# Three borders between four programs of a fused decoder: later clearing of semaphores, one meeting of the engines, last stores waited for in the next program

## The chip, the cores and the metric

The kernel runs on one core of a Trainium2 chip. The core has five engines with an instruction stream of their own: PE (matrix products), DVE (vector), ACT (scalar), POOL (GpSimd) and SP, which here only issues DMAs. They agree by semaphores. The metric is the device time of one launch in microseconds (us), median of several runs. Beside it stands one profiled execution, whose span goes from the first to the last instruction on the core.

## The reference

A decoder of two layers on x of 8 x 512 x 256 in float32. Each sublayer is added to its input and normalised:

```python
x = _layernorm(x + _L0_attn_ref(x, ...))    # recurrent mixer with weights mixed by a router
x = _layernorm(x + _L0_xattn_ref(x, ctx_1024, ctx_1024, ...))   # 16 heads, pruned columns
x = _layernorm(x + _L0_ffn_ref(x, ...))     # 8 experts, top 2, capacity 1024
x = _layernorm(x + _L1_attn_ref(x, ...))    # gated linear attention with decay
x = _layernorm(x + _L1_xattn_ref(x, ctx_1024, ctx_1024, mask, ...))
x = _layernorm(x + _L1_ffn_ref(x, ...))     # 8 experts, all computed, weighted by a gate
```

The expert layer writes each token to a slot of a table `buf` of 8 x 1024 rows, runs the experts over the table and gathers two result rows for each token.

## The kernel before

`decoder` runs four programs one after the other: `stage_front` (the mixer of layer 0, and q, k and v of the cross attention), `stage_attend_route` (attention, routing, scatter into `buf`, and a fallback path), `stage_experts` (16 units of 512 table rows) and `stage_tail` (all of layer 1). Tiles and semaphores are named with the prefixes front, xa, ex and ta. Each program is a `Block` with one hand-written instruction stream for each engine. Its streams end in a branch, and the block ends in a **meeting**: every engine drains (waits until its own work is done), reports to POOL, and goes on when POOL releases it. So no engine starts the next program until the last one is there.

A `Room` holds one program's tiles and semaphores. Its `clear` (L30 to L34) is called when the program's context is left, after the block: POOL resets the program's semaphores to zero (L33), and a second meeting of all engines follows (L34). Only then do the streams of the next program start. There are three such borders, and the same two steps once more at the end of the kernel.

SP's stream ends each program with waits on DMAs. What matters here:

- `stage_front`, L226 to L229: the loads `ahead_ld`, the zeroing of `buf` (`zero_st`), the stores of x1 (`x1_st`) and the stores of q, k and v (`qkv_st`). The last q and k parts leave from `w_all`, where the next program keeps the tile `early`; v leaves from `late`.
- `stage_attend_route`, L858 to L862: loads for later (`k_ld`), stores of x2, stores of the fallback rows (`fo_st`, from the tile probs) and POOL's scatters (`sent`).
- `stage_experts`, L1564: the stores of the expert outputs (`st`, 16 units in two buffers) to the table `results`.
- `stage_tail`, L1858: the stores of the output.

The first work behind each border: in the attention program SP loads the second chunk of q and k, L88 (the first lies in `late` already), PE makes scores (L1347), DVE and ACT take maxima and exponentials (L1076, L979), POOL normalises (L909), PE transposes (L1360), and `copy_tile` (L740 on DVE, L742 on ACT) moves the transposed tiles to `early` for the first eight heads. In the expert program PE first makes two weight products (L1689) while SP loads table rows (L1550), x2 and fallback rows of sequence 0 (L1554, L1555). In the tail PE transposes x3 (L2296), SP loads x2 and fallback rows of sequence 1 and the contexts (L1832 to L1838), and POOL gathers the result rows of sequence 1 by eight indirect DMAs (`gather(1)`, L1866).

The order inside each engine's stream is written out by hand; nothing is scheduled.

## Time and profile before

| what | us |
|---|---|
| median of 3 runs | 1961.33 (1960.6 to 1966.12) |
| the profiled execution's own time | 1966.77 |
| its span | 1964.7 |
| PE busy in the span | 1783.4 (91%) |
| DVE busy | 1264.8 (64%) |
| ACT busy | 991.4 (50%) |
| POOL busy | 639.4 (33%) |
| mean granted clock of PE | 0.970 of full |

The profiled execution took 2.1 us more than its span, and 5.4 us more than the median. The borders lie at about 238 to 249, 1011 to 1016 and 1374 to 1380 us. PE is busy nearly all the time between them. Rows that end in a bracket give the idle time before the row and what ended it. A name ending in q (SPq, POOLq) is the sequencer of that engine, where waits, drains and DMA issues are recorded.

### The profile page before, as it was taken

To read this page: it belongs to the slowest core of one execution; us is meant where nothing else is said; L and a number is where in the kernel's file an instruction comes from. 1 tells how busy PE (TensorE), PEld (TensorE's weight loads), DVE (VectorE), ACT (ScalarE), POOL (GpSimd) and SP (SyncE) were. 2 spreads that over 40 slices of the span, in tenths; PEclk is the share of its full clock that TensorE was granted. 3 is DMA by queue.
4 is the path that set the end of the run, shared out by engine and by line. 5 is a ranking of instruction groups with operands and counts; after the bars stand their busy time and mean duration, and the time that the engine had idled before them with its cause. 6 is when DMAs were issued, how large, how long until landed. Compare 5 with 4: busy or idle time off the path is not lost. (4 is left out here: it accounts for less than half of the span.)

```text
span 1964.7 us, 26168 instructions
## 1 busy us (share of the span) xinstructions
PE 1783.4 (91%) x8373; PEld 1058.0 (54%) x8373; DVE 1264.8 (64%) x2933; ACT 991.4 (50%) x2603; POOL 639.4 (33%) x813
## 2 busy tenths in 40 slices
PE   7999868989889898888869999999678999999997
PEld 5556534455445454544445566566455665666553
DVE  2686558888989999898411211221566878786665
ACT  4336689999989898997321111111232333233220
POOL 2000055555667666666310001000541324221100
PEclk9999989999999999999889999999788999999999
DMA  5248821212222222321662334431411111100000
GB/s 215 86 169 277 261 86 44 60 54 70 82 55 83 78 79 66 81 81 65 226 212 82 132 107 139 147 111 54 150 60 59 35 58 49 49 12 17 11 12 21
DMA packets 164071, 183.29 MB, mean 93 GB/s; under 512 B 19652, under 2 KB 143803, under 8 KB 162912
## 3 DMA queue, kind: packets, MB, share of 16 engines
q1 hardware_dynamic: 157792, 165.46, 26.4%
q0 software_dynamic: 6144, 16.18, 2.6%
q8 instruction: 67, 1.10, 0.2%
q14 instruction: 68, 0.56, 0.1%
HBM read 119.01 MB, written 63.18 MB: 93 GB/s over the span
## 5 line engine op out<-in xcount | busy, mean ns | idle before, releaser
L909 POOL TENSOR_SCALAR xa_probs<-xa_probs,xa_small 128x512 f32<-128x512 f32 x512 | 344.8, 690 | 242.0 <-DVE xa_small L1070 241.9
L979 ACT ACTIVATE xa_probs<-xa_ps_s,xa_small 128x512 f32<-128x512 f32 x512 | 360.9, 742 | 40.7 <-DVE xa_small L1076 36.1
L1076 DVE TENSOR_REDUCE xa_small<-xa_ps_s 128x2 f32<-128x1024 f32 x256 | 309.1, 1208 | 41.2 <-PE xa_ps_s L1347 41.2
L1360 PE MATMUL xa_ps_t<-xa_ident,xa_probs 128*128 128x128 f32 x2048 | 308.3, 283 | 17.1 <-DVE early L740 7.1
L1360 PEld LDWEIGHTS xa_ps_t<-xa_ident,xa_probs 128*128 128x128 f32 x2048 | 229.5, 142 | 151.9 <-ACT early L742 44.4
L2442 PE MATMUL ta_ps_e<-late,ta_x5T 128*128 128x512 f32 x512 | 235.8, 594 | 1.4 <-DVE ta_acc L2195 1.4
L1347 PE MATMUL xa_ps_s<-xa_k,xa_q 96*128 96x512 bf16 x496 | 151.4, 387 | 54.0 <-ACT xa_probs L979 52.4
L1610 ACT ACTIVATE ex_hid<-ex_ps_g 128x512 f32<-128x512 f32 x64 | 38.2, 597 | 275.7 <-PE ex_ps_u L1709 272.9
L2195 DVE SCALAR_TENSOR_TENSOR ta_acc<-ta_ps_e,ta_gate,ta_acc 128x256 f32<-128x256 f32 x256 | 123.5, 483 | 67.4 <-PE ta_ps_e L2442 60.8
L1665 DVE TENSOR_TENSOR ex_hid<-ex_hid,ex_ps_u 128x512 f32<-128x512 f32 x64 | 44.0, 687 | 184.5 <-ACT ex_hid L1610 179.0
L2442 PEld LDWEIGHTS ta_ps_e<-late,ta_x5T 128*128 128x128 f32 x512 | 93.9, 189 | 96.8 <-issue 84.0
L742 ACT ACTIVATE early<-xa_ps_t 128x512 f32<-128x512 f32 x216 | 135.4, 652 | 8.1 <-PE xa_ps_t L1360 7.6
L742 ACT ACTIVATE late<-xa_ps_t 128x512 f32<-128x512 f32 x216 | 134.0, 653 | 8.4 <-PE xa_ps_t L1360 8.4
L979 ACT ACTIVATION_READ_ACCUMULATOR xa_probs<-xa_ps_s,xa_small 128x1 f32 x512 | 133.6, 261 | 0.0
L1709 PE MATMUL ex_ps_g<-ex_xsT,early 128*128 128x512 f32 x256 | 121.9, 599 | 2.3 <-ACT ex_xsT L1593 2.3
L1709 PE MATMUL ex_ps_u<-ex_xsT,early 128*128 128x512 f32 x256 | 120.3, 592 | 0.0
L1719 PE MATMUL ex_ps_d<-early,ex_hid 128*128 128x256 f32 x512 | 113.4, 379 | 0.1
L1719 PEld LDWEIGHTS ex_ps_d<-early,ex_hid 128*128 128x128 f32 x512 | 96.0, 190 | 13.3 <-DVE ex_hid L1665 0.5
L1347 PEld LDWEIGHTS xa_ps_s<-xa_k,xa_q 96*128 96x128 bf16 x496 | 33.9, 99 | 125.9 <-ACT xa_probs L979 85.3
L1866 POOL DMA_INDIRECT ta_rows<-scratch_results,route_i x56 | 54.9, 980 | 90.7 <-POOLq L34 74.8
L1674 DVE COPY ex_out<-ex_ps_d 128x1024 f32<-128x1024 f32 x16 | 19.6, 1224 | 98.2 <-PE ex_ps_d L1719 98.2
L1709 PEld LDWEIGHTS ex_ps_u<-ex_xsT,early 128*128 128x128 f32 x256 | 48.8, 191 | 61.6 <-issue 61.6
(371 smaller groups left out, 3047.5 us busy)
## 6 DMA issues: line engine op xcount, KB each, us to landing
scratch_qk_parts<-front_w_all SPq DMA_DIRECT2D x16, 768.0 KB, 5.7
xa_q<-scratch_qk_parts SPq DMA_DIRECT2D x186, 64.0 KB
xa_k<-scratch_qk_parts SPq DMA_DIRECT2D x186, 64.0 KB
scratch_buf<-late SPq DMA_DIRECT2D x8, 1024.0 KB, 5.3
early<-in_L_ffn_Wg SPq DMA_DIRECT2D x16, 512.0 KB
early<-in_L_ffn_Wu SPq DMA_DIRECT2D x16, 512.0 KB
early<-in_L_ffn_Wd SPq DMA_DIRECT2D x16, 512.0 KB
ex_xs<-scratch_buf SPq DMA_DIRECT2D x16, 512.0 KB, 5.3
```

Of the source, the lines that this page charges most:

```text
L742: eng.activation(dst, src, ACT.Copy, accum_out=out).then_inc(copied[t], 1)
L909: ins = pool.tensor_scalar(probs[n % NP][:, t, :], probs[n % NP][:, t, :], rinv[n % 2][:, t:t + 1], 1.0, ALU.mult, ALU.mult)
L979: ins = act.activation(probs[n % NP][:, t, :], ps_s[j][:, t % 2, :], ACT.Exp, bias=nmax[n % 2][:, t:t + 1], accum_out=rsum[n % 2][:, t:t + 1])
L1076: dve.tensor_reduce(nmax[n % 2][:, 2 * j:2 * j + 2], ps_s[j][:, :, :], AX.X, ALU.max, negate=True).then_inc(max_up, 1)
L1347: ins = pe.matmul(ps_s[j][:, t % 2, :], q_[:, n % CH, t * P:(t + 1) * P], keys[:, n % CH, :], start=True, stop=True)
L1360: ins = pe.transpose(ps_t[t % 2][:, i * P:(i + 1) * P], probs[m % NP][:, i, t * P:(t + 1) * P], ident[:, :])
L1665: dve.tensor_tensor(hid[m % 2][:, j, :], hid[m % 2][:, j, :], ps_u[j % 2][:, :], ALU.mult).then_inc(hid_up, 1)
L1709: ins = pe.matmul(ps[:, :], wt[:, h, j * P:(j + 1) * P], xsT[u][:, h, :], start=(h == 0), stop=(h == DH - 1))
L1719: ins = pe.matmul(ps_d[:, t, :], hid[u][:, j, t * P:(t + 1) * P], wd[u][:, j, :], start=(j == 0), stop=(j == FT - 1))
L1866: pool.indirect_dma_start(out=rows[b % 2][:, n, t, :], out_offset=None, in_=a["results"], in_offset=bass.IndirectOffsetOnAxis(ap=route_i[: ...
L2195: dve.scalar_tensor_tensor(acc[c % 2][:, t, :], ps_e[n % 2][:, i, :], gate[c % 2][:, t, e:e + 1], acc[c % 2][:, t, :], ALU.mult, ALU.add). ...
L2442: ins = pe.matmul(ps_e[n % 2][:, :, :].rearrange("p e d -> p (e d)"), x5T[c % 2][:, h, t * P:(t + 1) * P], ew[:, h, e:e + 2, :].rearrange( ...
```

## The change

- `Room` no longer clears on leaving. `clear` only resets the semaphores, with no meeting after it, and is called one program later: POOL clears front's semaphores as its last instruction in the attention program, and the attention program's as its last in the expert program. The tail registers two clears that run when it is left, for its own and for the expert program's semaphores, with no meeting between or behind them.
- SP's last waits on `qkv_st`, `fo_st` and `st` are taken out of the three programs. They stand in the next program ahead of what needs them: `qkv_st` ahead of the first copies to `early` (ACT and DVE, `m == 0`) and ahead of SP's store of `fw`; `fo_st` ahead of SP's load of the fallback rows and ahead of ACT's first Gelu; `result_st` on POOL ahead of `gather(1)`.
- The other waits at the end of the programs stay.

```diff
     def __init__(self, nc, ctx, stage):
         self.nc, self.ctx, self.stage, self.sems = nc, ctx, stage, []
-        ctx.callback(self.clear)
     def clear(self):
         self.nc.clear_and_free_semaphores(self.sems)
-        self.nc.all_engine_barrier()
...
             sp.wait_ge(zero_st, 16 * B)
             for u in range(2):
                 sp.wait_ge(x1_st[u], 16 * B // 2)
-                sp.wait_ge(qkv_st[u], 48 * B // 2)
...
             g, hp = m // HU, m % HU
+            if m == 0:
+                for u in range(2):
+                    eng.wait_ge(k.qkv_st[u], 48 * B // 2)
...
                 if b == 0:
+                    for u in range(2):
+                        sp.wait_ge(k.qkv_st[u], 48 * B // 2)
                     sp.wait_ge(fn_up, 2 * DH)
...
             for u in range(2):
                 sp.wait_ge(x2_st[u], 16 * B // 2)
-                sp.wait_ge(fo_st[u], 16 * B // 2)
                 sp.wait_ge(sent[u], 16 * 2 * T * B // 2)
...
             pool.tensor_copy(k.bvw[:, :, :], col(k.bv[:, :]).to_broadcast([P, DH, P]))
+            k.front.clear()
...
             sp.dma_start(x2[:, :, :], tok(a["x2"][0])).then_inc(x2_ld, 16)
+            for u in range(2):
+                sp.wait_ge(k.fo_st[u], 16 * B // 2)
             sp.dma_start(fb[:, :, :], tok(a["fallback"][0])).then_inc(x2_ld, 16)
...
-            for u in range(2):
-                sp.wait_ge(st[u], 16 * NU // 2)
...
             pool.tensor_tensor(rstd[:, :], ve[:, :], k.mhalf[:, :], ALU.pow).then_inc(m_root, 1)
+            k.attend.clear()
...
                 wait(act, d_up, m - 1)
+                if m == 0:
+                    for u in range(2):
+                        act.wait_ge(k.fo_st[u], 16 * B // 2)
...
         r = Room(nc, ctx, "ta")
+        ctx.callback(k.expert.clear)
+        ctx.callback(r.clear)
...
+            for u in range(2):
+                pool.wait_ge(k.result_st[u], 16 * E)
             gather(1)
```

What stands in a row on the engines. Semaphores of a cleared program are used again, and these lists give a semaphore the name of its first owner: front_x_ld2 and front_x_ld3 are `st` of the expert program, and barrier_..._gather and _release are the two halves of a meeting.

SP at the first border. Before:

```order
L195 DMA scratch_qk_parts<-front_w_all 128x6x512
L198 DMA scratch_v<-late 128x4x256 [waits front_v_up]
L97 UNCONDITIONAL_BRANCH [waits front_qkv_st0,front_x1_st1,front_x1_st0,front_qkv_st1,front_zero_st,front_ahead_ld]
L750 UNCONDITIONAL_BRANCH [waits barrier_Pool_Activation_PE_DVE_SP_release]
L88 DMA xa_q<-scratch_qk_parts 16x4x512 x6
L88 DMA xa_k<-scratch_qk_parts 16x4x512 x6
```

Now:

```order
L195 DMA scratch_qk_parts<-front_w_all 128x6x512
L198 DMA scratch_v<-late 128x4x256 [waits front_v_up]
L95 UNCONDITIONAL_BRANCH [waits front_x1_st0,front_x1_st1,front_zero_st,front_ahead_ld]
L754 UNCONDITIONAL_BRANCH [waits barrier_Pool_Activation_PE_DVE_SP_release]
L86 DMA xa_q<-scratch_qk_parts 16x4x512 x6
L86 DMA xa_k<-scratch_qk_parts 16x4x512 x6
```

The two waits on the q, k and v stores are gone from the branch; no DMA has changed its place.

POOL from the end of the attention program, through the expert program, to the tail's gather (ISA is the clearing of semaphores). Before:

```order
L966 COPY late<-late 128x256
L653 UNCONDITIONAL_BRANCH
L33 ISA [waits barrier_Pool_Activation_PE_DVE_SP_gather]
L1566 UNCONDITIONAL_BRANCH [waits barrier_Pool_Activation_PE_DVE_SP_gather]
...
L1583 TENSOR_TENSOR ex_rstd<-ex_ve,late 128x4 [waits front_inv_up]
L1524 UNCONDITIONAL_BRANCH
L33 ISA [waits barrier_Pool_Activation_PE_DVE_SP_gather]
L1860 UNCONDITIONAL_BRANCH [waits barrier_Pool_Activation_PE_DVE_SP_gather]
L1866 DMA ta_rows<-scratch_results,route_i 128x256 x8
```

Now:

```order
L971 COPY late<-late 128x256
L32 ISA
L652 UNCONDITIONAL_BRANCH
L1574 UNCONDITIONAL_BRANCH [waits barrier_Pool_Activation_PE_DVE_SP_gather]
...
L1591 TENSOR_TENSOR ex_rstd<-ex_ve,late 128x4 [waits front_inv_up]
L32 ISA
L1530 UNCONDITIONAL_BRANCH
L1874 UNCONDITIONAL_BRANCH [waits barrier_Pool_Activation_PE_DVE_SP_gather]
L1880 DMA ta_rows<-scratch_results,route_i 128x256 [waits front_x_ld2,front_x_ld3]
L1880 DMA ta_rows<-scratch_results,route_i 128x256 x7
```

Each clearing has moved from between two meetings to ahead of the only one, and the gather has got the wait on the last result stores.

POOL at the end of the kernel. Before:

```order
L1870 TENSOR_TENSOR ta_rx<-ta_vex,late 128x4 [waits front_k_up]
L1870 TENSOR_TENSOR ta_rg<-ta_veg,late 128x4 [waits ta_g_var] x2
L1750 UNCONDITIONAL_BRANCH
L33 ISA [waits barrier_Pool_Activation_PE_DVE_SP_gather]
```

Now:

```order
L1884 TENSOR_TENSOR ta_rx<-ta_vex,late 128x4 [waits xa_fT_ld1]
L1884 TENSOR_TENSOR ta_rg<-ta_veg,late 128x4 [waits front_x1_st0] x2
L1762 UNCONDITIONAL_BRANCH
L32 ISA [waits barrier_Pool_Activation_PE_DVE_SP_gather]
L32 ISA x2
```

One clearing instruction has become three, since the numbers of the two programs' semaphores no longer lie in one range.

## Rows read from the trace of the kernel before

**Rows 1.** The page, busy time of each engine.

```profile
PE 1783.4 (91%) x8373; PEld 1058.0 (54%) x8373; DVE 1264.8 (64%) x2933; ACT 991.4 (50%) x2603; POOL 639.4 (33%) x813
```

**Rows 2.** Timeline, border 1: start, length, engine, line, what, [idle before it].

```profile
240.33 1.22 DVE L386 TENSOR_TENSOR late<-front_ps_o,late 128x1024 f32<-128x1024 f32 x1
...
241.57 1.11 SPq L198 DMA_DIRECT2D scratch_v<-late  x1
...
249.36 1.87 PE L1347 MATMUL xa_ps_s<-late 96*128 96x512 bf16 x4 [11.56 <-PEq L34]
```

**Rows 3.** Waits of SP's sequencer: us in total, times, longest.

```profile
SPq L229 <- DMA scratch_v<-late: 5.1, 1, 5.1
...
SPq L1564 <- DMA scratch_results<-ex_out: 2.5, 1, 2.5
...
SPq L861 <- DMA scratch_fallback<-xa_probs: 2.4, 1, 2.4
```

**Rows 4.** Source L97, border 1: PE released by the first meeting (ns, start us).

```profile
L97 PEldq EVENT_SEMAPHORE  x1: 51/51/51, 248.4 to 248.4; - x1
```

**Rows 5.** Source L33, all four clearings: ns min/median/max, first and last start us.

```profile
L33 POOLq DRAIN  x4: 113/166/176, 248.4 to 1963.8; - x4
L33 POOLq EVENT_SEMAPHORE_RANGE_CLEAR  x4: 178/407/457, 248.6 to 1964.0; - x4
```

**Rows 6.** Timeline, border 2.

```profile
999.68 12.54 SPq L782 DMA_DIRECT2D scratch_fallback<-xa_probs  x4
...
1016.23 3.75 PE L1689 MATMUL ex_ps_d<-late 128*128 128x256 f32 x8 [5.51 <-PEq L34]
```

**Rows 7.** Source L653, border 2: POOL's drain, PE's release by the first meeting.

```profile
L653 POOLq DRAIN  x1: 6400/6400/6400, 1006.1 to 1006.1; - x1
...
L653 PEldq EVENT_SEMAPHORE  x1: 51/51/51, 1015.2 to 1015.2; - x1
```

**Rows 8.** Timeline, border 3.

```profile
1379.65 1.94 PE L2296 MATMUL ta_ps_w<-late 128*128 128x128 f32 x8 [5.28 <-PEq L34]
1380.34 1.02 POOL L1866 DMA_INDIRECT ta_rows<-scratch_results,route_i  x1 [74.83 <-POOLq L34]
```

**Rows 9.** Source L1524, border 3: PE's release by the first meeting.

```profile
L1524 PEldq EVENT_SEMAPHORE  x1: 51/51/51, 1379.0 to 1379.0; - x1
```

**Rows 10.** Timeline, the tail's first step.

```profile
1390.40 2.35 POOL L1881 TENSOR_TENSOR ta_x3b<-late 128x1024 f32<-128x1024 f32 x1
...
1391.82 1.91 DVE L2075 TENSOR_TENSOR ta_g<-ta_g 128x4 f32<-128x4 f32 x1 [2.72 <-ACT ta_g L1928]
...
1396.64 3.37 DVE L2052 SCALAR_TENSOR_TENSOR ta_z<-ta_rows,route_w,ta_z 128x256 f32<-128x256 f32 x8
```

**Rows 11.** Timeline, the tail's second step.

```profile
1416.47 0.95 POOL L1866 DMA_INDIRECT ta_rows<-scratch_results,route_i  x1 [0.30 <-issue]
...
1419.25 8.93 DVE L2052 SCALAR_TENSOR_TENSOR ta_z<-ta_rows,route_w,ta_z 128x256 f32<-128x256 f32 x8 [7.25 <-DMA ta_rows<-scratch_results,route_i]
...
1428.09 0.15 DVE L2075 TENSOR_TENSOR ta_g<-ta_g 128x4 f32<-128x4 f32 x1
```

**Rows 12.** Windows: length, busy us (instructions) by engine, then PEclk, DMA share, GB/s.

```profile
1020.00:1022.00 2.00, 2.00 (x7) 1.79 (x8) 0.00 (x0) 0.00 (x0) 0.00 (x0) 0.56 1.05 351
1026.00:1028.00 2.00, 0.52 (x5) 0.28 (x3) 0.00 (x0) 2.00 (x10) 0.00 (x0) 1.00 0.00 0
1028.00:1030.00 2.00, 1.20 (x2) 0.71 (x3) 0.00 (x0) 1.94 (x3) 0.00 (x0) 0.64 0.03 8
1441.00:1443.00 2.00, 0.00 (x0) 0.00 (x0) 1.77 (x4) 0.84 (x4) 1.81 (x2) 1.00 0.00 0
```

**Rows 13.** Windows of the attention program's start, same columns.

```profile
261.00:263.00 2.00, 2.00 (x9) 1.47 (x9) 0.82 (x1) 1.38 (x5) 1.29 (x2) 0.50 0.00 0
```

**Rows 14.** Timeline there: first copy to `early`, first scores from the loaded chunk.

```profile
259.75 0.69 DVE L740 TENSOR_SCALAR_CACHE_REDUCE early<-xa_ps_t 128x512 f32<-128x512 f32 x1 [0.36 <-PE xa_ps_t L1360]
...
266.39 0.59 PE L1347 MATMUL xa_ps_s<-xa_k,xa_q 96*128 96x512 bf16 x2 [0.34 <-ACT xa_probs L979]
```

More of the change, by code:

```diff
@@ L88, in load_half, with stage_front @@
         eng.dma_start(dst[g * DK:(g + 1) * DK, :, :], src.rearrange("(h d) s -> d h s", d=DK)).then_inc(done, 16)
-def stage_front(nc, a, late):
+def stage_front(nc, a, late, k):
     KC = P // E
@@ L98, in stage_front @@
         r = Room(nc, ctx, "front")
+        k.front = r
         w_all = r.sb("w_all", [P, B, DH, 3 * D])
@@ L165, in stage_front @@
         ahead_ld = r.sem("ahead_ld")
+        k.qkv_st = qkv_st
         buf = a["buf"].rearrange("(n p r) d -> n p (r d)", p=P, r=2048 // D)
@@ L654, in stage_attend_route @@
         r = Room(nc, ctx, "xa")
+        k.attend = r
         probT = [room[:, :].rearrange("p (j t s) -> p j t s", t=T, s=S) for room in (early, late)]
@@ L721, in stage_attend_route @@
         fo_st = [r.sem(f"fo_st{u}") for u in range(2)]
+        k.fo_st = fo_st
         k_ld, k_pad = r.sem("k_ld"), r.sem("k_pad")
@@ L1525, in stage_experts @@
         r = Room(nc, ctx, "ex")
+        k.expert = r
         xs = [r.sb(f"xs{j}", [P, T, D]) for j in range(3)]
@@ L1539, in stage_experts @@
         st, w_ld = ([r.sem(f"{n}{u}") for u in range(2)] for n in ("st", "w_ld"))
+        k.result_st = st
         t_up, xsT_up, gu_up, gelu_up, hid_up, d_up, out_up = (r.sem(n) for n in
@@ L2534, in decoder @@
         k = Later(nc, ctx, late)
-        stage_front(nc, a, late)
+        stage_front(nc, a, late, k)
         with ExitStack() as inner:
```

## The prediction

> **What bounds the kernel now.** The page comes first: PE is busy for 91% of the span, no other engine for more than 64% [rows 1]. Between the borders some engine is full all the time, so what shortens a border is not filled again from elsewhere, unless a program's first steps absorb it. The timeline then shows three stretches in which PE stands still: 11.56, 5.51 and 5.28 us, 22.4 us together [rows 2, 6, 8]. That is all that a change of the borders can take. Third, SP's waits say what part of each stretch is the landing of the last stores: 5.1, 2.4 and 2.5 us [rows 3]. Last, the first meeting's release and the next program's first instruction give what the clearing and the second meeting cost.
>
> **The second meeting and the clearing.** At border 1 PE is released by the first meeting at 248.4 and starts at 249.36 [rows 4, 2]; at border 2 at 1015.2 and 1016.23 [rows 7, 6]; at border 3 at 1379.0 and 1379.65 [rows 9, 8]. With 0.1 us left for a release and a first instruction, this part gives 0.85, 0.9 and 0.55 us. It goes whole, for nothing runs beside it.
>
> **Border 1, the stores of q, k and v.** SP arrives last: it issues the last store until 241.57 + 1.11 = 242.7 and then waits 5.1 us for landing [rows 2, 3]. The next to arrive is DVE, whose last operation ends at 240.33 + 1.22 = 241.55 [rows 2]. So without the wait SP is still the last, at 242.7, and the whole 5.1 us go. SP's other waits there showed no time. Sum 5.1 + 0.85 = 5.95; with the second landed semaphore's own instruction 6.0.
>
> The wait moves ahead of the first copies to `early`. DVE makes the first at 259.75 [rows 14], 10.4 us after the border; with the border ending at 243.3 that is 253.7, and the stores landed by 242.7 + 5.1 = 247.8. Cover of 5.9 us, so zero wait; ACT's copies stand behind its own waits, and behind them ACT's exponentials of the next head. Two waits each for the three copies on ACT: at most 0.05 us each by the only semaphore row near [rows 4], 0.3 us together; since each is already met, I take 0.1 for all added waits and keep 0.3 as the end.
>
> SP now issues the second q/k chunk (12 loads) at 243.3, behind stores still moving. Before, all DMA was quiet from 261 on [rows 13], at most 11.7 us after the issue, and PE needs the chunk at 266.39, 17.0 us after [rows 14]. If the chunk had to wait for all the rest of the stores (247.8 - 243.3 = 4.5 us), it would be there after 16.2 us: still 0.8 us early. So zero, bounded above by a few tenths to some us if the two streams disturb each other (the rival of the starts).
>
> By the Trainium skill's page "DMA: Bandwidth & Descriptors", section "Queues, rings and completion order", a DMA's completion increment lands only after every earlier write of that DMA engine. This speaks against the change: the chunk cannot be reported before the stores in front of it. That is the 16.2 us just worked out from rows; by the page too the sum stays as it is.
>
> **Border 2, the fallback stores.** Here another engine is close behind. SP issues until 999.68 + 12.54 = 1012.2 [rows 6], and POOL's drain runs from 1006.1 for 6.4 us to 1012.5 [rows 7]. So POOL becomes the last to arrive, and the clearing of front's semaphores now stands in its stream ahead of the meeting: one more drain and a clearing, 0.17 + 0.41 = 0.6 us [rows 5]. POOL is there at 1013.1 instead of SP at about 1014.7: release at about 1013.3 against 1015.2, 1.9 us. With 0.9 for the second meeting 2.8 us. Bounds: 2.2 if the drain grows with it; 3.3 if POOL's long drain isn't real work and SP at 1012.2 sets the time. What the new waits on `fo_st` cover: the stores land at 1012.2 + 2.4 = 1014.6, SP asks after four loads, ACT later still. Nothing is queued behind them but the fallback load, which the expert program needs only in its units 10 to 12.
>
> **Border 3, the result stores.** SP's wait of 2.5 us goes [rows 3]; DVE's last copy had ended before SP could issue the store, so SP stays last. With 0.55 us: 3.05 us for PE, DVE, ACT and SP. Not for POOL: its gather now waits for the same stores. Before, it began at 1380.34, 0.69 us after the others [rows 8]. The stores land at about 1378.6, so it begins at about 1379.3: 1.0 us earlier. In the first step DVE takes the gathered rows at 1396.64 without having waited [rows 10]. In the second step the rows are there 1419.25 - (1416.47 + 0.95) = 1.8 us after the last gather was issued [rows 11]. Eight gathers of 0.95 + 0.30 = 1.25 us [rows 11] from 1380.34 end at 1390.4, so the rows landed at 1392.2: 4.4 us of slack. After the change DVE comes 3.05 earlier and the rows 1.0, so slack 2.4 us is left. No wait.
>
> There is a second order effect. DVE's `ta_g`, 128 x 4 elements, takes 1.91 us at 1391.82 and 0.15 us a step later; it ends 1.0 us after POOL's 2.35 us addition of `x3b`, which was running when it began [rows 10, 11]. With DVE 3.05 us earlier and POOL 1.0, `ta_g` comes at 1388.8, before `x3b` (1389.4), and is short: up to 1.76 us more. But the first step's other POOL work moves by 1.0 only, and the step's reading needs it. So the chain gains between 0 and 1.76 here; I take 0.8, near the middle. This gives 3.85 for border 3, with 1.0 as the low end if POOL sets the step, and 4.8 as the high.
>
> By the Trainium skill's page "SBUF — State Buffer", section "SBUF: two separate sides", POOL and DVE share a port pair that one of them locks for a whole instruction. The trace's 1.91 against 0.15 us agrees; taken alone the page would give the full 1.76, 1 us more than my sum.
>
> **The end.** One drain and clearing becomes three clearings, and the meeting behind it goes. The last clearing starts at 1964.0 and takes at most 0.46 [rows 5]; the span ends at 1964.7, so the meeting was 0.25. Added: two clearings of 0.41 and a drain of 0.17, 1.0. Net cost 0.75, between 0.1 (two short clearings of 0.18) and 1.1.
>
> **The sum.** 6.0 + 2.8 + 3.85 - 0.75 - 0.1 = 11.8 us against the profiled execution's 1966.8, which lies 5.4 us above the median. The terms are waits, whose length doesn't hang on that difference, so I take them off the median: 1961.3 - 11.8 = 1949.5.
>
> **The rivals.**
>
> *The clock stays up.* After each border PE runs at half clock (1.2 GHz of 2.4). In the expert program this lasts from the start at 1016.23 until about 1021.8, where the window has 0.56 [rows 12]: 5.5 us of full PE work, of which half would be saved, 2.8 us. After the change PE is idle for 5.5 - 2.8 = 2.7 us there and 2.2 us at border 3. Rows show both outcomes for such a gap: idle from 1026.5 to 1028.8 it fell to half (0.64 in that window), idle from 1441 to 1443 it stayed at 1.00 [rows 12]. At border 3 the transposes are short and PE waits again at once, so I count border 2 only. Time 1949.5 - 2.8 = 1946.7.
> The Trainium skill's page "TensorE: Matmul & The Clock Gate", section "Why this matters for your kernels", asks only for the absence of long idle gaps, and by it both gaps would be harmless. The trace agrees in one of two cases.
>
> *The starts absorb it.* The tail's first step goes at POOL's pace (1.0 us in place of 3.85), and the disturbed chunk at border 1 comes up to 2 us late. For it: POOL's chain of gather and additions is close behind; against it: the slack above. Time 1949.5 + 2.85 + 2 = 1954.3.
>
> *The wait hid something else.* While the engines stand in the meetings, their sequencers may fetch the next program's code; the stretch would then stay, under another name. It would do less than it says: only the second meetings go, 0.85 + 0.9 + 0.55, less 0.85 at the end, 1.5 us: 1959.8. Against it: after a release first instructions start within 0.1 us on all engines, and with it speaks only that this is all the trace can show.
>
> *Slower.* The stores of border 1 land late, because the chunk's loads and the fetches of constants share the DMA engines with them, and ACT, in order, stands at its first copy with all exponentials behind it. This costs nothing until 253.7 and 1 us per us from there on. To end 0.3% above the median it has to eat the 11.8 us and 5.9 more: landing at 271.4, 24 us late, for stores on which SP waited 5.1 us. Time then 1967.2. I see nothing for it but that it can't be excluded.
>
> **The numbers.** Forecast 0.45, clock 0.27, absorbed 0.18, hidden fetch 0.07, slower 0.03. What a measurement tells from no change is 0.3%, 5.9 us: 1955.4 to 1967.2. The first three are faster, 0.90; hidden fetch is within, 0.07; slower 0.03. For 8 in 10 the range takes the forecast with its ends (border 2 by 0.6 and 0.5, border 3 by 1.0 up, the end by 0.6), the clock case with the same ends below (1946.7 - 2.2 = 1944.5), and the absorbed case above (1954.3, and 0.7 for it): 1944.5 to 1955.0.
>
> **What would show it.** Right: PE's idle time at the borders is about 5.6, 2.7 and 2.2 us; SP's waits on the stores at the borders are gone; no wait longer than 0.1 us appears at the first copies, and POOL waits about 2.2 us ahead of the gather; `ta_g` takes 0.15 us. Border 2's last arrival is POOL's drain and clearing. Wrong: a new idle time of PE ahead of the first scores from the loaded chunk (the starts absorb it), of DVE ahead of the first gathered rows, or a gap between the release and the first instruction of a program (hidden fetch). The forecast is wrong above all if the tail's first step doesn't follow PE.

## The result, and the profile after

| | before | after |
|---|---|---|
| runs, median (lowest to highest), us | 1965.45 (1960.60 to 1966.12), 5 runs | 1951.64 (1948.85 to 1954.16), 5 runs |
| ratio, 95% interval | | 0.9939 [0.9923, 0.9955] |
| profiled execution, us | 1966.8, span 1964.7 | 1951.64, span 1949.8 |
| mean granted clock of the profiled execution | 0.970 | 0.974 |

The change makes the kernel faster by 0.6%, 12.0 us by the ratio. The forecast was 11.8 us less, 1949.5 us. The two medians differ by 13.8 us, and the forecast's time had been taken off an earlier median of the kernel before, 1961.3 us, which is 1965.45 with two more runs: so the measured time lies 2.1 us above the forecast time, though the gain is as forecast.

The page first, as in [rows 1]. PE's busy time is 1.3 us less of 1783.4, and the span 14.9 us shorter; what went is mostly idle time.

```profile
PE 1782.1 (91%) x8373; PEld 1056.6 (54%) x8373; DVE 1263.1 (65%) x2933; ACT 991.4 (51%) x2603; POOL 639.8 (33%) x813
```

Timeline at border 1, which answers to [rows 2]:

```profile
241.69 1.11 SPq L198 DMA_DIRECT2D scratch_v<-late  x1
...
243.40 4.80 SPq L86 DMA_DIRECT2D xa_q<-scratch_qk_parts  x6
...
243.44 1.86 PE L1353 MATMUL xa_ps_s<-late 96*128 96x512 bf16 x4 [5.53 <-PEq L95]
```

PE's idle time went from 11.56 to 5.53 us. SP has issued its last store by 242.80 and PE runs 0.64 us later: neither a landing nor a second meeting is left. SP then issues the next loads beside its own stores, and that takes 4.80 us where it took 2.67 before, as this row of the timeline before shows:

```profile
249.33 2.67 SPq L88 DMA_DIRECT2D xa_q<-scratch_qk_parts  x6
```

No engine waited for it: the first scores from a loaded chunk start at 260.55, 5.84 us earlier than before, and stood idle for 0.34 us, on ACT:

```profile
260.55 0.59 PE L1353 MATMUL xa_ps_s<-xa_k,xa_q 96*128 96x512 bf16 x2 [0.34 <-ACT xa_probs L985]
```

Timeline at border 2 and the drains there, which answer to [rows 6, 7]:

```profile
1000.58 3.59 SPq L786 DMA_DIRECT2D scratch_fallback<-xa_probs  x2
...
1004.79 1.53 PE L1701 MATMUL ex_ps_d<-late 128*128 128x256 f32 x6 [2.13 <-PEq L652]
```

```profile
L652 POOLq DRAIN  x1: 46/46/46, 999.6 to 999.6; - x1
...
L652 SPq COMPARE_BRANCH  x1: 33/33/33, 1004.4 to 1004.4; - x1
```

PE's idle time went from 5.51 to 2.13 us. POOL arrives at 999.6, SP at 1004.4: the engine that I had put last is there 4.8 us ahead. The windows show the second difference. The clock is full from PE's first product on, where [rows 12] had half clock until 1021.8.

```profile
1004.00:1008.00 4.00, 3.21 (x17) 2.93 (x18) 0.21 (x2) 1.49 (x2) 0.58 (x1) 1.00 0.82 238
1008.00:1014.00 6.00, 4.37 (x29) 3.82 (x27) 0.00 (x0) 2.52 (x10) 0.00 (x0) 1.00 1.05 349
1362.00:1364.00 2.00, 1.61 (x8) 1.28 (x8) 0.00 (x0) 0.00 (x0) 0.00 (x0) 0.68 0.77 240
```

(The columns are the stretch and its length, busy time of PE, PE's weight loads, DVE, ACT and POOL, then granted clock, DMA share, GB/s.) The third row is border 3: there the clock falls too, 0.3 us after PE's first instruction, though the idle time is as short as at border 2 (2.10 us). And at border 2 the full clock doesn't last: at PE's next short idle time, ahead of its first transposed rows, it falls, and the product takes 3.59 us, as it did before (3.53).

```profile
1014.66 3.59 PE L1721 MATMUL ex_ps_g<-ex_xsT,early 128*128 128x512 f32 x4 [2.29 <-ACT ex_xsT L1602]
```

Timeline at border 3 and in the tail's first step, which answers to [rows 8, 10]:

```profile
1361.58 0.37 SPq L1568 DMA_DIRECT2D scratch_results<-ex_out  x1
...
1362.39 1.66 PE L2312 MATMUL ta_ps_w<-late 128*128 128x128 f32 x8 [2.10 <-PEq L1530]
...
1365.68 1.02 POOL L1880 DMA_INDIRECT ta_rows<-scratch_results,route_i  x1 [74.25 <-DMA scratch_results<-ex_out]
...
1373.69 0.15 DVE L2091 TENSOR_TENSOR ta_g<-ta_g 128x4 f32<-128x4 f32 x1
...
1374.50 0.95 POOL L1880 DMA_INDIRECT ta_rows<-scratch_results,route_i  x1 [0.30 <-issue]
...
1375.47 2.36 POOL L1897 TENSOR_TENSOR ta_x3b<-late 128x1024 f32<-128x1024 f32 x1
...
1378.91 1.19 PE L2356 MATMUL ta_ps_o<-ta_aT,late 128*128 128x128 f32 x4 [3.60 <-POOL ta_risen L1907]
...
1380.26 3.38 DVE L2068 SCALAR_TENSOR_TENSOR ta_z<-ta_rows,route_w,ta_z 128x256 f32<-128x256 f32 x8 [4.08 <-DMA ta_rows<-scratch_results,route_i]
```

PE's idle time went from 5.28 to 2.10 us. POOL gathers 3.29 us after PE's start, and two new waits stand here: PE's 3.6 us on POOL, DVE's 4.08 us on gathered rows. A little later PE's output product takes almost twice what it took before at the same place (1.99 us).

```profile
1382.92 3.78 PE L2366 MATMUL ta_ps_w<-late,ta_oT 128*128 128x256 f32 x8 [0.69 <-ACT ta_oT L1951]
```

From PE's first instruction of the tail to the last store it takes 582.88 us in place of 580.68: 2.2 us were given back.

At the end, the clearings, which answer to [rows 5], and SP's last wait:

```profile
L32 POOLq DRAIN  x3: 65/98/148, 1948.7 to 1949.5; - x3
L32 POOLq EVENT_SEMAPHORE_RANGE_CLEAR  x3: 68/178/416, 1948.8 to 1949.7; - x3
```

From the issue of the last store to the end of the span it takes 4.53 us and took 4.37.

So two questions stood: is the clock at border 2 the work of the shorter gap or luck of the run, and did the tail give back its 2.2 us to POOL's pace (a rival of my prediction) or to the clock?

### The profile page after: what moved, and what is told of

Same layout as the page of the kernel before. It is cut to its first block and busy times, and to the rows that moved or that the text cites. A ratio compares the mean times of both kernels' runs of the same rounds, so it can differ in the third digit from the quotient of the medians.

```text
span 1949.8 us, 26129 instructions
## 1 busy us (share of the span) xinstructions
PE 1782.1 (91%) x8373; PEld 1056.6 (54%) x8373; DVE 1263.1 (65%) x2933; ACT 991.4 (51%) x2603; POOL 639.8 (33%) x813
```

## The experiments

Three comparisons (the first figure of a name), each with five rounds beside the kernel before, and each on another chip. All kernels start from the changed one; the second comparison has no run of it unaltered. "Idle" is PE's idle time at borders 1, 2, 3. "Expert" is from PE's first product of the expert program to that of the tail, less the idle time at border 3; "attention" likewise up to border 2. "Product" is the tail's first output product; "tail" is from PE's first instruction there to the last store.

| kernel | ratio [95%] | idle | attention | clock at the expert's start | expert | product | tail |
|---|---|---|---|---|---|---|---|
| before | 1 | 11.56, 5.51, 5.28 | 761.4 | 0.50 for 5.5 us | 358.1 | 1.99 | 580.7 |
| after | 0.9939 [0.9923, 0.9955] | 5.53, 2.13, 2.10 | 759.2 | 1.00 | 355.5 | 3.78 | 582.9 |
| e1_again | 0.9932 [0.9913, 0.9951] | 5.53, 2.13, 2.10 | 770.5 | 1.00 | 353.9 | 3.78 | 584.5 |
| e1_meetings_only | 0.9989 [0.9978, 1.0] | 10.70, 4.63, 4.69 | 770.4 | 0.50 for 4.7 us | 359.2 | 3.78 | 582.8 |
| e1_stores_only | 0.9934 [0.9913, 0.9954] | 5.86, 2.46, 2.43 | 761.8 | 1.00 | 353.9 | 3.78 | 581.3 |
| e1_x3b_first | 0.9911 [0.9893, 0.993] | 5.53, 2.13, 2.10 | 760.6 | 1.00 | 353.9 | 1.99 | 581.0 |
| e2_undo_b1 | 0.9959 [0.9945, 0.9972] | 10.71, 2.13, 2.10 | 761.5 | 1.00 | 353.9 | 3.78 | 584.7 |
| e2_undo_b2 | 0.9962 [0.9948, 0.9976] | 5.52, 4.63, 2.10 | 763.0 | 0.50 for 6.0 us | 358.5 | 3.78 | 584.0 |
| e2_undo_b3 | 0.9931 [0.9918, 0.9945] | 5.52, 2.13, 4.70 | 762.9 | 1.00 | 355.3 | 3.78 | 584.5 |
| e2_warm | 0.992 [0.9906, 0.9933] | 5.53, 2.13, 2.10 | 764.3 | 1.00 | 353.9 | 1.99 | 581.4 |
| e3_again | 0.9929 [0.9915, 0.9944] | 5.52, 2.13, 2.10 | 770.6 | fell after 1.2 us | 357.2 | 1.99 | 580.6 |
| e3_keep_b2 | 0.9944 [0.9927, 0.9961] | 5.52, 2.44, 2.10 | 766.2 | 0.50 for 3.0 us | 355.4 | 3.78 | 584.2 |
| e3_undo_b3 | 0.994 [0.9923, 0.9957] | 5.52, 2.13, 4.69 | 762.9 | 1.00 | 353.9 | 3.78 | 582.3 |
| e3_best | 0.9922 [0.9908, 0.9936] | 5.52, 2.13, 2.10 | 763.2 | 1.00 | 353.9 | 1.99 | 581.5 |

The column of the expert program holds two falls of the clock that must be kept apart. One is at its start, at border 2. The other comes 10 to 12 us into it, at PE's idle time of 2.28 us ahead of its first transposed rows: there the product takes 3.4 to 3.8 us in before, after, e1_meetings_only, e2_undo_b2, e2_undo_b3 and e3_again, and 1.95 or 1.96 in the other eight. With neither fall the program takes 353.9 us (seven profiles), with the second alone 355.5 and 355.3, with the first alone 355.4 (e3_keep_b2), with both 357.2 to 359.2.

**The control, twice.** The changed kernel unaltered.

> The changed kernel once more, unaltered, as the control of the three others and to see what differs from one profile to the next. Theory A (the meetings and store waits give a fixed time, and the clock at border 2 is luck of the run): time 1950 to 1953 us, PE idle 5.5, 2.1 and 2.1 us at the three borders again, while the granted clock just after border 2 may be high or low, and the 2 us by which the attention program was shorter inside need not come again. Theory B (the shorter gap at border 2 always keeps the clock up): 1.00 granted through the first products of the expert program in every profile. In both, POOL's first gather starts 3.0 to 3.5 us after PE's first instruction of the tail.

> The changed kernel once more, as the control of the three others of this comparison. Expected: 0.9930 to 0.9940 of the kernel before, PE idle 5.53, 2.13 and 2.10 us at the borders, clock up at the start of the expert program.

The idle times are the same to 0.01 us in three profiles, and the gather starts 3.29, 3.31 and 3.30 us after PE. The granted clock at the start of the expert program is 1.00 in two, and in the third it falls after PE has begun:

```profile
1015.00:1016.00 1.00, 0.73 (x4) 0.69 (x5) 0.00 (x0) 0.77 (x1) 0.00 (x0) 1.00 0.80 274
1016.00:1017.00 1.00, 1.00 (x5) 0.86 (x4) 0.22 (x2) 0.72 (x2) 0.00 (x0) 0.72 0.97 246
1017.00:1018.00 1.00, 1.00 (x6) 0.82 (x4) 0.00 (x0) 0.00 (x0) 0.58 (x1) 0.50 1.02 287
```

The first control's time, 1956.1 us, is above the 1950 to 1953 expected, and the kernel before beside it is higher as well (1968.9). Theory B of the first expectation (always up) fell, and the expectation of the second on the clock as well. The attention program took 759.2, 770.5 and 770.6 us in three profiles of one kernel: so the 2.1 us by which it was shorter after the change are no more than profiles of one kernel differ by. The windows of its last stretch show one thing that such differences go with, the granted clock, first in the first profile of the changed kernel, then in e1_again (the last columns: granted clock, DMA share, GB/s):

```profile
850.00:995.00 145.00, 126.32 (x721) 69.64 (x722) 99.20 (x323) 83.76 (x232) 79.51 (x105) 0.98 0.47 155
```

```profile
850.00:995.00 145.00, 126.78 (x700) 68.90 (x699) 98.44 (x322) 81.83 (x227) 79.41 (x105) 0.92 0.42 135
```

**Meetings alone, stores alone.** First, the three waits on the last stores stand again at the programs' ends:

```diff
                 sp.wait_ge(x1_st[u], 16 * B // 2)
+                sp.wait_ge(qkv_st[u], 48 * B // 2)
 ...
+                sp.wait_ge(fo_st[u], 16 * B // 2)
 ...
+            for u in range(2):
+                sp.wait_ge(st[u], 16 * NU // 2)
```

> The late clearing and the single meeting stay; the three waits on the last stores stand again at the end of each program. Theory (the sum's parts add): only the second meetings' time goes, 0.85 + 0.9 + 0.55 us, less 0.15 at the end: 2.1 us under the kernel before (about 1963 where that is 1965). PE idle 10.6, 4.6 and 4.7 us. SP waits 5.1, 2.4 and 2.5 us on the stores. Rival 'clock': with the gap at border 2 at 4.6 us the granted clock falls there as before; if it stays up, the time is 2.8 us shorter still. Rival 'hidden fetch' expects the same time as the changed kernel, since the store waits would have covered something else.

Second, only the second meeting comes back, at each of the three borders:

```diff
     with ExitStack() as ctx:
+        ctx.callback(nc.all_engine_barrier)
         r = Room(nc, ctx, "front")
```

> The stores are waited for in the next program and the clearing stays late, but the engines meet a second time at each of the three borders. Theory: the second meeting costs 0.25 to 0.9 us at each border, so 1.2 to 2.3 us above the changed kernel (about 1953 to 1954) and 10 to 12 below the kernel before. The spread tells whether the 0.85 us between release and start came from the meeting itself (then 2.0 or more comes back) or from the clearing and drain of POOL ahead of it (then under 1). Rival 'hidden fetch': no gain over the kernel before beyond 2 us. Rival 'clock': the gap at border 2 is 2.4 to 3.0 us; if the clock falls with it the time is 2.8 us longer.

Meetings alone: 0.9989, 2.2 us, as the sum said, but the interval reaches from 0 to 4.3 us. The store waits carry the rest: with them moved and the second meeting back, 13.0 us are gone, where the control has 13.4. The rival of the hidden fetch falls, for it left no more than 2 us to this kernel. The idle times split the border's own cost. The second meeting adds 5.86 - 5.53 = 0.33 us at each border. Against before, meetings alone saves 0.86, 0.88 and 0.59 us; what is left over those 0.33 is 0.53, 0.55 and 0.26 us, the drain and clearing that [rows 5] show.

**One store wait at a time.** Each of the three lines above alone.

> The changed kernel with one wait put back: at the end of the first program SP waits again for the stores of q, k and v. Theory (the 5.1 us of landing stood wholly on the path): PE idle 10.6 to 10.8 us at border 1 in place of 5.53, and 5.1 us above the changed kernel; borders 2 and 3 as in the changed kernel (2.13 and 2.10 us idle, clock up after border 2). Rival 'the starts absorb it': less than 5.1, because in the changed kernel the second chunk of q and k, issued in 4.8 us in place of 2.7 beside the stores, held up PE later in the attention program by what would now come back.

> The changed kernel with one wait put back: at the end of the attention program SP waits again for the last fallback stores. Direct cost 2.5 us (PE idle about 4.6 us at border 2 in place of 2.13). Theory 'clock': with that gap the granted clock is at half in the first 5 us of the expert program, as in the two profiles with 4.6 and 5.5 us, and the expert program from PE's first to its last instruction is 3 to 4.5 us longer: 5.5 to 7 us above the changed kernel. Rival: the clock there is luck of the run (it was up in four profiles with 2.1 to 2.5 us): then 2.5 us.

> The changed kernel with one wait put back: at the end of the expert program SP waits again for the result stores. Direct cost 2.5 us (PE idle 4.6 us at border 3), and POOL's first gather is then 0.7 us after PE's first instruction and not 3.3. Theory 'POOL's pace': the first step of the tail gives back what its later gather had cost, 2.2 us, so only 0.3 us above the changed kernel. Theory 'clock': the 2.2 us went into half clock in the tail's first step (the product of w and oT took 3.78 us there and 1.99 before); then the wait costs its 2.5 us whenever the clock is down at that product in both kernels.

> Once more the changed kernel with SP's wait on the result stores put back at the end of the expert program, now beside the changed kernel itself. In the two profiles with that wait (4.7 us idle) the tail's first step is no shorter than without it, measured from PE's first instruction (second transposes after 30.0 us, against 29.4 to 29.7). So if the step is set by PE's own chain and the clock, the wait costs its whole 2.6 us: ratio to the kernel before 0.0013 above the control's. If POOL's later gather gave the gain back, the two are the same within 0.5 us.

PE's idle time grows by 5.18, 2.50 and 2.60 us. In time, against the mean of the two controls' ratios (0.9930): 5.6 us for border 1 and 6.2 us for border 2; for border 3 0.2 us in one comparison and, against its own control, 2.2 in the other, each uncertain by some 3 to 4 us. Border 1's wait stood wholly on the path, and its expectation came true. Border 2's seems to cost more than its gap: in the profile the clock falls with it, and the expert program is 4.6 us longer than with no fall at all. Only part of this is the fall at the border. The second fall is in this profile too, as it is in the first profile of the changed kernel, where nothing fell at the start; against that one the program is 3.0 us longer.

```profile
1011.50 3.75 PE L1702 MATMUL ex_ps_d<-late 128*128 128x256 f32 x8 [4.63 <-PEq L652]
```

```profile
1011.00:1015.00 4.00, 3.50 (x8) 2.86 (x9) 0.21 (x2) 1.49 (x2) 0.58 (x1) 0.50 0.54 178
```

Border 3 is the test of POOL's pace. With the wait back, POOL gathers 0.73 us after PE in place of 3.30, yet the second transposes start 29.97 and 29.14 us after PE's first instruction, against 29.38 and 29.55 without it, at half clock in all four. The tail takes 584.5 and 582.3 us against 582.9 and 584.5. So no cost of POOL's later gather shows in the profiles. The test moves two things, though: with the wait back `ta_g` is long again (3.05 and 2.88 us, beside POOL's `x3b`; 0.15 without it). And the times can't decide it: 0.2 us is what theory "POOL's pace" expected of this wait, 2.2 is near the 2.5 of theory "clock".

**Is it the gap?** Border 2 with its wait back, and PE made busy in the wait:

```diff
                 down(c)
+            for _ in range(20):
+                pe.transpose(ps_s[0][:, 0, 0:P], ident[:, :], ident[:, :])
```

> The kernel with SP's wait on the fallback stores put back at border 2, and at the end of PE's part of the attention program 20 transposes of the identity that nobody reads, some 2.6 us of PE work in time in which PE stood still. Nothing that others wait for moves. Theory 'the gap's length sets the clock': PE idle at border 2 falls from 4.6 to about 2.0 us with the wait still there, the clock stays at 1.00 in the first 5 us of the expert program, its first product takes 1.97 us and not 3.75, and the expert program is 4 to 5 us shorter than with the wait alone: about 2.5 us above the changed kernel, where the wait alone measured 0.9962 of the kernel before. Rival 'the clock comes from something else that the wait moves' (the DMA traffic or the other engines' start): the clock falls at that border and the time stays 5.5 to 6 us above the changed kernel.

```profile
1008.11 2.35 PE L1522 MATMUL xa_ps_s<-xa_ident 128*128 128x128 f32 x20
1012.90 1.62 PE L1704 MATMUL ex_ps_d<-late 128*128 128x256 f32 x3 [2.44 <-PEq L652]
```

Neither theory is met. The gap is short again, but the clock fell, 0.4 us before PE's first product:

```profile
1011.50:1012.50 1.00, 0.00 (x0) 0.00 (x0) 0.00 (x0) 0.00 (x0) 0.00 (x0) 1.00 0.37 124
1012.50:1012.90 0.40, 0.00 (x1) 0.03 (x1) 0.00 (x0) 0.04 (x1) 0.00 (x0) 0.55 0.00 0
1012.90:1013.40 0.50, 0.50 (x1) 0.47 (x2) 0.00 (x0) 0.50 (x1) 0.00 (x0) 0.50 0.00 0
```

It stayed down for 3.0 us of PE's work, not 6.0, and the expert program is 3.1 us shorter than with the wait alone (355.4 against 358.5), some 1.5 us of it because the second fall didn't come. In time it lies 3.0 us above its control. The windows of the other profiles tell why one case can't settle it. After PE's last product the fall came 4.2 us later before the change, 3.8 in e2_undo_b2, 2.5 in e1_meetings_only, 2.1 here and 3.3 in e3_again, there with PE at work again. A gap of 4.6 us or more lies behind all these times: half clock at PE's first product in three of three, for 4.7 to 6.0 us of work. One of 2.13 to 2.46 us ends ahead of nearly all of them: the clock stayed up in nine of eleven and fell for some 3 us in two. So at border 2 the shorter gap goes with a rarer and shorter fall; it doesn't exclude it, and what picks the moment is open.

The length of the gap can't be all, as border 3 shows. There the gap is 2.10 to 2.43 us in ten profiles, and in all ten the clock fell, 0.3 to 1.1 us after PE's first instruction of the tail; in the four with 4.69 us or more it fell in the gap. The work behind the gap differs: in the first profile PE is busy for the whole of the first 3.81 us at border 2 and for 2.70 us at border 3, where it waits again after eight short transposes. No run varied this, so it is not shown to be the reason.

```profile
1363.00:1364.00 1.00, 1.00 (x5) 0.64 (x4) 0.00 (x0) 0.00 (x0) 0.00 (x0) 0.50 1.03 306
```

**The tail's first step.** One edit aims at POOL, the other at the clock. The addition of `x3b` for sequence 0 goes ahead of POOL's wait:

```diff
+            pool.tensor_tensor(x3b[:, :, :], x3[0][:, :, :], row(m_bo[:, :]).to_broadcast([P, T, D]), ALU.add).then_inc(m_x3b, 1)
             for u in range(2):
                 pool.wait_ge(k.result_st[u], 16 * E)
```

> The changed kernel, but in the tail POOL makes the addition x3b of sequence 0 before it waits for the result stores and gathers, so that this addition (2.35 us) stands in time in which POOL only waited. Theory A (POOL sets the pace of the tail's first step: wait 3.3 us, then 8 gathers, then x3b, then the risen sums that PE reads): the chain from border 3 to the first attention's end is 2.2 to 2.4 us shorter, so about 2.3 us under the changed kernel (1949.3 where that is 1951.6), PE's wait for the risen sums goes from 3.6 us to about 1.2. Theory B (DVE's wait on the gathered rows, 4.1 us, sets the step): the gain is under 0.5 us, since the landing of the gathered rows doesn't move.

And PE is kept busy in three of its idle times there:

```diff
             def m_outer(b):
+                if b == 0:
+                    warm(12)
 ...
             def m_reading(b):
+                if b == 0:
+                    warm(22)
```

> The changed kernel with transposes of the identity that nobody reads (12, 22 and 36 of them) in three idle times of PE in the tail's first steps: ahead of the outer products, ahead of the reading of sequence 0, ahead of the transposes of sequence 1. Theory 'clock' (what the tail's first step gave back is half clock at the output product and at the products behind it): the clock stays up, the output product takes 1.99 us and not 3.78, and the second transposes start 28.0 to 28.2 us after PE's first instruction of the tail in place of 29.4; the tail is 2 to 3 us shorter. Theory 'POOL's pace': PE waits for the risen sums and DVE for the gathered rows as before, and the tail's length stays within 0.3 us.

| | rows landed, DVE starts on them | output product | second transposes | product behind them |
|---|---|---|---|---|
| before | 16.99, no wait | 21.18, full clock | 27.94 | 33.05 |
| after | 17.87 | 20.53, half clock | 29.38 | 35.38 |
| e1_again | 17.87 | 20.70, half clock | 29.55 | 35.62 |
| e3_again | 17.35 | 20.81, full clock | 27.87 | 32.93 |
| e1_stores_only | 17.28 | 20.15, half clock | 28.70 | 33.67 |
| e1_x3b_first | 17.75 | 18.69, full clock | 28.24 | 33.31 |
| e2_warm | 17.70 | 19.07, full clock | 28.19 | 33.40 |

(us after PE's first instruction of the tail.) The moved addition did what it was to do for PE: the output product starts 2 us earlier. Nothing came of it: DVE turns to that product only after the gathered rows, 23.21 us in, and the second transposes start at 28.24. The control with nothing moved, but with the product at full clock, reaches them at 27.87. So theory A of the first expectation fell: its 2.3 us did not come by POOL. In time the kernel was 4.1 us below its control, a difference within the noise of the two. The 2.2 us that the tail gave back go with the half clock at the output product and behind it. Over all fourteen profiles the second transposes start 27.9 to 28.4 us in where the product has full clock (five) and 28.7 to 30.0 where it has half (nine), the next product at 32.9 to 33.6 and 33.7 to 36.0. That of e1_stores_only is the best of the nine, and its tail of 581.3 us is as short as some at full clock, so the one product doesn't fix the tail's length. The product and DVE behind it, at full clock in e3_again:

```profile
1395.35 1.99 PE L2366 MATMUL ta_ps_w<-late,ta_oT 128*128 128x256 f32 x8 [0.69 <-ACT ta_oT L1951]
...
1397.39 1.23 DVE L2118 TENSOR_TENSOR ta_z<-ta_ps_w,ta_x3b 128x1024 f32<-128x1024 f32 x1
```

With the idle transposes the product ran at full clock and the step came as expected (28.19), and the tail is 1.5 us shorter than in the first profile, 3.1 shorter than in e1_again and 0.8 longer than in e3_again (2 to 3 shorter had been expected). But one profile of the unaltered kernel has that too, so a single profile doesn't prove that they held the clock. Over all profiles the product is at full clock in three of three with idle transposes or the moved addition, in one of three of the changed kernel itself, in none of the seven with a meeting, a wait or transposes elsewhere put in, and in the one of before.

**All of it together**, with the expert program's semaphores cleared in POOL's own stream:

```diff
-        ctx.callback(k.expert.clear)
 ...
             for s_ in range(B + 3):
                 step(s_)
+            k.expert.clear()
```

> The changed kernel with three edits in the tail: POOL's addition x3b of sequence 0 ahead of its wait for the result stores; idle transposes on PE ahead of the outer products, of the reading and of the second transposes (10, 18 and 44); the expert program's semaphores cleared at the end of POOL's own stream, not after the last meeting. Alone, the first measured 0.9911 and the second 0.9920 of the kernel before, where the changed kernel had 0.9932. Theory: both aim at the same first step, whose next bound is DVE's wait for the gathered rows (they land 17.4 to 17.9 us after PE's first instruction); so they don't add. With the second transposes at 28.2 us, now and the next product at full clock, tail 580 to 581 us, and the end 0.3 shorter: 2.5 to 4 us under the control. Rival: the effects add, 5 us or more.

0.9922 against the control's 0.9929, medians 1953.58 and 1955.48 us: 1.4 to 1.9 us less, where 2.5 to 4 had been expected; this comparison can't tell it from nothing. That the effects don't add fits the profile (second transposes at 28.35 us, DVE at 17.86 on the rows). The end is shorter by 0.37 us (4.16 from the last store's issue to the end, 4.53 after the change). The three versions with edits in the tail's work have the lowest ratios of all, 0.9911, 0.9920 and 0.9922, but their intervals all overlap the controls'.

## Why the prediction was right

- **Border 1, 6.0 us: right.** Idle time fell by 6.03 us, and undoing it costs 5.18 us of idle time and 5.6 of time. The moved waits cost nothing: no idle time on stores stands at the first copies. The chunk was issued more slowly (4.80 us in place of 2.67 for its first six loads) and nobody waited for it.
- **Border 2, 2.8 us: the term was mis-sized, 3.38 us.** The step that failed is "POOL becomes the last to arrive". Where [rows 7] had a drain of 6.4 us, there were 1.26 us in the clearing and 0.05 us in the meeting after the change, and POOL was there 4.8 us ahead of SP. I had the right value as my other bound, 3.3. What made the drain of before last 6.4 us, I can't say.
- **Border 3, 3.85 us: 3.18 at PE's start; the 0.8 for `ta_g` didn't come.** `ta_g` is short, 0.15 us, as predicted (and 2.41 to 3.05 in the three profiles with the wait back), but DVE then waits for the gathered rows. The step "slack 2.4 us is left" failed: the rows could be used 4.8 us after POOL's last gather (1380.26 less 1374.50 + 0.95), where I had taken the second step's 1.8 us from [rows 11], and the gather began 3.29 us after PE's start where my times gave 2.7. In the control at full clock (e3_again) DVE still comes to the output product 0.36 us earlier than before, 22.85 us in against 23.21, just as that product ends. Of this, 0.3 us go in a pause between two of DVE's next operations that the trace before doesn't have (the row below), and the second transposes start 0.07 us earlier. So 3.18 is the term by PE's idle time; in time, undoing the wait there cost 0.2 and 2.2 us, and its gain alone is not shown.

```profile
1400.62 0.25 DVE L1742 BATCH_NORM_AGGREGATE ta_mvb<-ta_st6b 128x2 f32<-128x6 f32 x2 [0.18 <-issue]
```

- **The end, 0.75 us: 0.16.** Three drains and clearings took 1.0 us by their rows, the span's end moved by 0.16; my low bound was 0.1. I had added the two long clearings, but two of the three were short (68 and 178 ns).
- **The sum by what was measured:** 6.03 + 3.38 + 3.18 - 0.16 = 12.4 us, against 11.8 forecast. The three ratios of the changed kernel give 12.0, 13.4 and 14.0 us. That the total is this close is in part luck: border 2 and the end were 0.6 us better each than forecast, border 3 0.7 worse, and outside the sum two effects of the clock nearly cancel in the first profile, 2.6 us gained in the expert program and 2.2 lost in the tail. With 2.1 us in the attention program, which the controls don't show, this makes up the span's 14.9 us.
- **The rival of the clock came in part, and its size was right for the fall that it named.** With the clock up at border 2 the expert program of the first profile takes 355.5 us and not 358.1: 2.6 us, where I had said 2.8. I had not counted the second fall, at the first transposed rows, which is worth 1.4 to 1.6 us by itself. It came in four of the five profiles with a fall at the start and in two of the nine without, so it may hang on the first, and then the shorter gap is worth up to 4.3 to 5.4 us; it isn't shown to, for the changed kernel had it in two profiles of three. The rows, of before and of e1_again:

```profile
1028.80 3.53 PE L1709 MATMUL ex_ps_g<-ex_xsT,early 128*128 128x512 f32 x4 [2.28 <-ACT ex_xsT L1593]
```

```profile
1025.50 1.96 PE L1721 MATMUL ex_ps_g<-ex_xsT,early 128*128 128x512 f32 x4 [2.28 <-ACT ex_xsT L1602]
```

- **The rival "the starts absorb it" named a loss that came by another cause.** The tail did give back 2.2 us in the first profile, about the size I had given (2.85), but with the clock and not by POOL's pace. In the control with the product at full clock nothing is given back (580.6 us against 580.7), with the gather 3.30 us behind PE.
- **Hidden fetch** and **slower** are out, by e1_stores_only and by the copies of border 1 that didn't wait.

The clock at border 2 stays up in two of the three profiles of the changed kernel, which would let one expect more than 12.4 us; its tail at half clock in two of three would let one expect less. Whether a difference is there can't be told: the ratios' intervals are about 3 us to either side, and the attention program alone differs by 11 us between profiles of one kernel.

The Trainium skill's page "TensorE: Matmul & The Clock Gate", section "Why this matters for your kernels", asks for the absence of long idle gaps. Here 4.6 us was long enough each time. Gaps of 2.1 to 2.5 us were short enough in nine profiles of eleven at border 2 and in none of ten at border 3. The rule is borne out in kind, but a short gap was no safeguard. The two contrary rows of the trace [rows 12] had kept me from putting it into the sum.

## What to carry to other kernels

Price a border by its parts, as PE's idle time shows them: the last store's landing (here 2.5 to 5.2 us), drain and clearing (0.3 to 0.55), a second meeting (0.33). Only the first is large, and it can be moved behind the next program's start wherever the stored data's next user comes later. Shorten a gap of PE and look at the clock behind it as well: the half speed behind a gap of 5 us cost 2.6 us here by itself, and up to 5.4 with the second fall. And before a step is put down to an engine's pace, look whether the same instruction has the same length in both traces; and take several profiles, for one alone can have the clock's luck.

## What was not expected of the hardware

- The granted clock of one kernel differs from run to run in the same stretch (0.98 and 0.92 over the attention program's last 145 us), and with it the attention program's length by 11 us, nearly the whole of this change's size. Five rounds still leave some 3 us.
- A drain can show a length that no work explains: 6.4 us for POOL at border 2 before, 46 ns in the meeting in the thirteen profiles with the moved clearing, behind a drain of 1.26 to 1.27 us after the same copies.
- DMA issue was slower with stores in flight: six loads took 4.48 to 4.82 us in the eleven profiles without the wait at border 1, 2.67 in the three with it.
- A gap of 2.1 us left the clock up at one border and not at the other, in the same kernel.
- Gathered rows came 4.8 us after the last gather, while the core's DMAs had moved 335 to 387 GB/s for some 10 us, and 1.8 us after it in the next step before the change, at 66 to 113 GB/s.
